# Low halves of the key and value weights made on GpSimd instead of VectorE, in a post-norm decoder layer on one core

## The reference, cut to what matters

```python
def _fp8_linear_pertensor(x, wq, w_scale, in_scale):
    xq = _div_clamp_fp8(x, in_scale)
    return jnp.einsum('bsi,oi->bso', xq * in_scale, wq) * w_scale
...
q = _fp8_linear_pertensor(ln_out, wq, wq_scale, q_in_scale).reshape(b, s, g, hpg, d)
k = _fp8_linear_pertensor(ln_out, wk, wk_scale, k_in_scale).reshape(b, s, g, d)
v = _fp8_linear_pertensor(ln_out, wv, wv_scale, v_in_scale).reshape(b, s, g, d)
...
qx = _fp8_linear_pertensor(ln_out, wqx, wqx_scale, qx_in_scale).reshape(b, s, g, hpg, d)
```

## Time and profile before

| | |
|---|---|
| median of 3 runs | 1780.35 us (1780.09 to 1781.36) |
| the profiled execution's own time | 1780.63 us |
| its span (first to last instruction) | 1778.5 us |
| PE / DVE / ACT / POOL busy | 98% / 79% / 62% / 15% of the span |
| granted TensorE clock | 0.997 of full speed over the span |
| one group in stage B (four pairs) | 153.17 us, of it PE busy 152.43 us |
| low halves, K and V, in stage B | 56 instructions of 0.34 us on DVE |

### The profile page before, as it was taken

One profiled execution on the slowest core, in us unless ns is written; L12 is line 12 of the kernel. 1 busy time (PEld: TensorE's weight loads), 2 busy tenths in 40 slices (PEclk: granted clock), 3 DMA queues, 4 the chain that ended last, 5 costly groups with the idle time before them and its releaser, 6 DMA issues.

```text
span 1778.5 us, 31332 instructions
## 1 busy us (share of the span) xinstructions
PE 1736.5 (98%) x10664; PEld 1180.9 (66%) x10664; DVE 1404.2 (79%) x4581; ACT 1103.9 (62%) x2378; POOL 273.9 (15%) x428
## 2 busy tenths in 40 slices
PE   9999999988999999999999999999999999989998
PEld 4454444666777777777777777777777777745453
DVE  1234526589888998998999899899889988879996
ACT  1252525375676767677776667767667665657775
POOL 0000000211121111112111111111111122101111
PEclk9999999999999999999999999999999999999999
DMA  8212200101101110121121012111101012000000
GB/s 284 83 59 83 71 24 26 37 1 50 50 19 42 45 62 19 44 68 36 33 67 32 19 44 67 37 44 55 32 19 44 32 48 97 1 1 19 25 25 30
DMA packets 45597, 83.30 MB, mean 47 GB/s; under 512 B 3585, under 2 KB 22529, under 8 KB 45057
## 3 DMA queue, kind: packets, MB, share of 16 engines
q1 hardware_dynamic: 45440, 81.31, 14.0%
HBM read 69.77 MB, written 10.49 MB: 45 GB/s over the span
## 4 chain that ended last, share of the span: by engine, by line
PE 63%; DVE 21%; issue 9%; ACT 3%; POOL 3%; DMA 1%; POOLq 0%; ACTq 0%
PE bank L536 13%; PE bank L602 9%; PE bank L648 8%; PE bank L701 5%; PE bank L626 4%; PE bank L737 3%; PE bank L455 3%; PE bank L493 3%; PE bank L581 2%; PE bank L407 2%; DVE nq L1250 2%; PE bank L434 2%; DVE nmx L1400 2%; DVE bnB L1226 2%; DVE pr L1260 2%
## 5 line engine op out<-in xcount | busy, mean ns | idle before, releaser
L536 PE MATMUL bank<-wqs,XQ 128*128 128x256 f16 x2048 | 246.4, 274 | 5.6 <-DVE x L1281 5.6
L602 PE MATMUL bank<-prT,KV 128*128 128x256 f32 x1024 | 245.3, 382 | 0.0
L648 PE MATMUL bank<-kT,qT 128*128 128x512 f32 x512 | 240.9, 593 | 0.0
L602 PEld LDWEIGHTS bank<-prT,KV 128*128 128x128 f32 x1024 | 189.3, 190 | 72.5 <-issue 51.9
L536 PEld LDWEIGHTS bank<-wqs,XQ 128*128 128x128 bf16 x2048 | 198.0, 99 | 47.7 <-DVE x L1281 21.1
L1020 ACT ACTIVATE pr<-bank,nmx 128x512 f32<-128x512 f32 x256 | 174.3, 687 | 57.4 <-DVE nmx L1400 56.0
L1569 POOL TENSOR_TENSOR rdev<-gvar,cst 128x7 f32<-128x7 f32 x128 | 193.1, 1509 | 10.0
L1567 POOL TENSOR_TENSOR gvar<-mvB,geps 128x7 f32<-128x7 f32 x128 | 30.7, 240 | 1040.2 <-DVE mvB L1240 1040.2
L1400 DVE TENSOR_REDUCE nmx<-bank 128x1 f32<-128x512 f32 x256 | 167.5, 682 | 9.6 <-PE bank L648 7.1
L821 ACT ACTIVATE prT<-bank 128x512 f32<-128x512 f32 x256 | 152.9, 613 | 26.7 <-PE bank L701 26.5
L701 PE MATMUL bank<-identf,pr 128*128 128x128 f32 x1024 | 151.6, 276 | 14.0 <-DVE pr L1260 11.0
(11 more groups left out here) (179 smaller groups left out, 3098.4 us busy)
## 6 DMA issues: line engine op xcount, KB each, us to landing
wst<-in_wcat SPq DMA_DIRECT2D x21, 512.0 KB, 4.0
nq<-in_wgu SPq DMA_DIRECT2D x16, 512.0 KB, 3.6
wpst<-in_wproj SPq DMA_DIRECT2D x8, 1024.0 KB, 6.3
wa<-in_wgu SPq DMA_DIRECT2D x16, 512.0 KB, 3.8
xT<-in_xT SPq DMA_DIRECT2D x4, 1024.0 KB, 7.7
nq<-in_wdn SPq DMA_DIRECT2D x8, 512.0 KB, 3.5
wkx<-in_wkvx SPq DMA_DIRECT2D x8, 512.0 KB, 4.9
tern_gu<-wa SPq DMA_DIRECT2D x16, 256.0 KB, 2.0
```

The source lines that it names most:

```text
L536: ins = mm(dst, XQ[:, b, c, k, j * P:(j + 1) * P], w, start=(k == 0 and m == 0), stop=(k == KT - 1 and m == 1))
L602: ins = mm(OB[:, 0:2 * P], KV[:, n % 2, t, P:2 * P], prT[:, st % 2, t, :, :].rearrange("p h s -> p (h s)"), start=(t == 0), stop=(t == ST ...
L648: mm(SB_[h][:], qT[:, h, st * P:(st + 1) * P], kT[:, :], start=True, stop=True).then_inc(s["scores_made"], 1)
```

## The change

DVE no longer makes any low half of K and V in stage B (parts 3g + 2 for g = 1 to 7; the three parts of group 0 are made ahead of the pairs on DVE as before). POOL makes them in pair b = 2, half 0 in step 2 and half 1 in step 3, each behind that step's `deviations`. POOL needs two instructions per tile where DVE needs one: a multiplication by `srel` in place in the staging buffer, then a subtraction of the fp16 high half into the fp16 low half. Between the four multiplications and the four subtractions stands a wait for its own instructions. Both engines raise the same count `wl_ready`.

```diff
--- before.py
+++ after.py
@@ DVE, pair @@
-                    if b == 2 and not last and st == 3:
-                        split_low(3 * (g + 1) + 2, 0)
                     if b in (1, 2) and not last and st == 1:
                         split_low(3 * (g + 1) + b - 1, 1)
                     if st == 0:
                         if T >= 2:
                             accumulate(T - 2, (4 * b - 2) % 16)
-                        if b and not last:
-                            split_low(3 * (g + 1) + b - 1, 1 if b == 3 else 0)
+                        if b in (1, 2) and not last:
+                            split_low(3 * (g + 1) + b - 1, 0)
@@ POOL @@
+            def split_low(part, half):
+                pool.wait_ge(s["wh_ready"], 2 * part + half + 1)
+                for c in WPART[part % 3]:
+                    for k in (2 * half, 2 * half + 1):
+                        own.do(g.tensor_scalar(staged(part, c, k), staged(part, c, k), srel[:, c, k:k + 1], None, ALU.mult))
+                own.sync()
+                for c in WPART[part % 3]:
+                    for k in (2 * half, 2 * half + 1):
+                        wh, wl = split_weights(part // 3, c, k)
+                        ins = g.tensor_tensor(wl, staged(part, c, k), wh, ALU.subtract)
+                ins.then_inc(s["wl_ready"], 1)
+
@@ POOL, pair @@
                     if nxt:
                         deviations(4 * n + 4 + st)
+                    if b == 2 and not last and st >= 2:
+                        split_low(3 * (gr + 1) + b, st - 2)
                     if T in XSTAT:
                         of_x(XSTAT[T])
```

## The result

The changed kernel takes 1775.94 us (median of 16 executions, 1774.54 to 1781.53) against 1780.36 us for the kernel before (16 executions, 1778.61 to 1784.74): ratio 0.9975, 95% interval 0.9968 to 0.9982. That is 0.25% or 4.4 us faster. A second measurement of the same code, further down, gave 0.9987 (0.9978 to 0.9996). The traces, whose pair times are steadier than the totals, show 3.7 us.

What follows compares the result with a forecast made beforehand. PE bounds the kernel, except where DVE's chain delays it ending pair b = 2. Gain min(0.58, 1.05 - 0.75) = 0.30 us per group, 7 x 0.30 = 2.1 us: 1778.2 us against the median 1780.35, range 1775.8 to 1788.0.

Steps and rivals of the forecast that it cites:

- Nothing is held: Rival: POOL's accesses slip between DVE's, up to 0.47 us delay per group; gain 4.2 us, 1776.1 us; chance 0.31.
- What bounds: End of pair b = 2: DVE's chain makes PE wait at L701; half 0 is on the path, half 1 covered.
- The cap: End of pair b = 2: gain limited by PE's idle 0.58 us per group, 4.2 us in all.
- some 0.7 us sooner: Pair b = 2: how much earlier pr ends, given the second nmx's wait for its score matmul and ACT's exponentials.
- the first rival: POOL's accesses slip between DVE's without holding it: gain 4.2 us, 1776.1 us; chance 0.31.
- d, the delay: DVE time lost to POOL's streams beside kn, pr, rounding: 0.75 us per group, bounds 0 and 3.5.
- nq's four follow each other too closely to be parted: Half 0, step 3: POOL's multiplications delay kn, pr and pr, 3 x 0.15 us, and not nq.
- POOL's sizes: POOL, each half: four multiplications of 0.29 us and four subtractions of 0.40, 2.8 us; 39 us over the kernel.
- cover: POOL time free before the next gvar: 4.0 us for half 0, 6.9 for half 1, against 2.8 needed.
- POOL's instructions are slow: Rival: from about 0.75 us each, rdev is late for nq; at 1 us each 8 us slower, 1788.5; chance 0.05.
- POOL holds the ports for a whole instruction: Rival: DVE blocked at nq, pr and rounding; at 1.8 us per group 5 us slower, 1785.5; chance 0.24.
- PE never waits for wlk: Next pair: half 1 is ready before PE's first wlk matmul at about 634.3, cover 6.9 us against 2.8.

Runs made afterwards that it cites:

- e3_half1_dve: Changed kernel with half 1 back on DVE in pair b = 3, step 0, half 0 staying on POOL: 1777.12 us, ratio 0.9985; pair b = 2 38.52 us.
- e2_half0_dve: Changed kernel with half 0 back on DVE in pair b = 2, step 3, half 1 staying on POOL: 1781.23 us, ratio 1.0002.
- e8_windows: Changed kernel, POOL started by DVE's progress: half 0 two wide instructions in step 3, half 1 four narrow multiplications and one wide subtraction: 1777.27 us, ratio 0.9980.
- e5_mult_tt: Changed kernel with POOL's multiplications as TENSOR_TENSOR, srel broadcast over the columns, instead of TENSOR_SCALAR: 1779.52 us (one execution); pair b = 2 39.16 us.
- e7_two_wide: Changed kernel with each half on POOL as two 128x512 instructions instead of eight of 128x128: 1792.89 us, ratio 1.0078.
- e4_sub_twice: Changed kernel with POOL doing the four subtractions of half 0 twice: 1780.3 us (one execution); pair b = 2 39.10 us.
- e11_after_again: The changed kernel measured again, nothing altered: 1778.33 us, ratio 0.9987 against the kernel before.
- e10_all_windows: Changed kernel, both halves as two wide POOL instructions started by DVE's progress, DVE's QX half 1 moved to step 0: 1774.39 us, ratio 0.9962.
- e6_mult_imm: Changed kernel with POOL's TENSOR_SCALAR multiplying by constant 1.0 instead of srel: 1776.94 us (one execution); pair b = 2 38.35 us.

## Why the prediction was right or wrong

The mechanism held; two of its sizes were off, and both errors made the gain too small. Forecast were 2.1 us, the traces show 3.7 and the first measurement 4.4. The result of 1775.94 us lies in the range by 0.14 us only and outside the forecast's own range (1776.6 to 1783.5); that it lies inside at all is partly luck, and so is the 0.7 us by which the first measurement exceeds the traces. It falls on the edge between the forecast and the rival "Nothing is held", whose edge was put at 0.54 us of delay per group; 0.53 or 0.54 were measured. But things are held: that rival's reason isn't what happened.

- **What bounds: right.** Only DVE's chain at the end of pair b = 2 was worth anything. Half 1's removal is worth nothing (e3_half1_dve has the full gain).
- **The cap: mis-sized.** The text had both limits: the second nmx that waits for the score matmul, "some 0.7 us sooner", and PE's idle time of 0.58, which it took because it was the smaller. The idle time understates what PE had to give (0.73 by the starts of L626 and L701), and the pair's cap was measured as 0.77. The forecast wasn't touched by it, the first rival was: with no delay at all the gain is 6 x 0.77 + (38.83 - 38.18) = 5.3 us, not 4.2.
- **d, the delay: mis-sized, and this is the term that decided.** Taken 0.75, measured 0.53. "nq's four follow each other too closely to be parted" failed: nq gave 0.26 of it, the largest part. pr gave 0.07 where two meetings at 0.15 stood. The rounding gave 0.21 for 0.2 forecast. Half 1 gave nothing for 0.1; where it meets nq at another distance it costs 0.10 to 0.14 (e2_half0_dve, e8_windows).
- **POOL's sizes: one right, one wrong.** The subtraction: 0.42 to 0.43 us for 0.40 forecast. The Trainium skill's "GPSIMD Engine Reference", section 3.1, had led to an estimate of 0.28 us for 128 columns of a two-input operation; the slopes below give 0.22 to 0.24, between that and the 0.20 taken. The multiplication: 0.71 for 0.29, taken from the affine select because that too has one tile in and one out. With one input it takes longer than with two, which no row before suggested. It did no harm: cover was 4.0 us, half 0 took 4.5, and behind the cover lay the slack of rdev, as the text had it. The rival "POOL's instructions are slow" named its point at 0.75 us for each instruction (by the cover of 4.0 and the slack of 2.8 us it would have been 0.85); the mean of the two kinds, (0.74 + 0.48) / 2 = 0.61, stayed under it.
- **"POOL holds the ports for a whole instruction": wrong for this kernel, right for one of its two instruction forms.** The changed kernel escapes it by accident. Its multiplications, which lie beside kn, nq and pr, are of the form that holds little (kn takes its usual 0.34 us wholly inside the first of them); its subtractions, of the form that holds all, mostly lie beside the statistics. e5_mult_tt exchanges the first form for the other, at the same distance from nq, and loses the gain; e7_two_wide makes the instructions long and is 0.78% slower. The Trainium skill's "SBUF — State Buffer", section "SBUF: two separate sides", says that of a VectorE instruction in a 2-port mode or with two SBUF inputs and a GpSimd one the first to start has the shared ports for the whole instruction; e7's kn (0.94 us, ending 0.08 us after POOL's) agrees for POOL's two-input instructions, but its first nq was held although its recorded start is 0.08 us ahead of POOL's; the changed kernel's nq (at most 473 ns beside multiplications of 599 ns and more) disagrees for the one-input form.
- **PE never waits for wlk**, as forecast. POOL, SP and PE at the end, from the timelines of the changed kernel:

```profile
629.48 2.00 POOL L1596 TENSOR_TENSOR wlk<-wst,whk 128x128 f16<-128x128 f32 x4
631.51 0.38 SPq L289 DMA_DIRECT2D wst<-in_wcat  x1
...
633.30 0.22 PE L536 MATMUL bank<-wlk,XQ 128*128 128x128 f16 x1
```

POOL is through at 631.48, PE's first matmul with the new wlk starts 1.8 us later. SP's load moves from 38.06 to 36.58 us into the pair, 1.5 us earlier and not 3 to 4, since the multiplications were longer. Nobody waits for it.

Left open is how a POOL TENSOR_SCALAR shares the ports with DVE. Both get longer when they meet (599 to 912 ns on POOL, 0.34 to at most 0.47 on DVE), and the price changes with the distance: the four nq take 1.11, 1.17, 1.25 or 1.37 us when the multiplications begin 0.29 (changed kernel, half 1), 0.13 (e4_sub_twice), 0.04 (e8_windows) or 0.41 us (changed kernel, half 0) ahead of them. The distance alone doesn't settle it: in the one pair of e11_after_again that strays they took 1.12 us at 0.41.

## What to carry to other kernels

Work moved from VectorE to GpSimd isn't priced by GpSimd's time but by what VectorE wants during it: here the same 4.4 us of GpSimd work a group cost VectorE's chain 2.9 us in one place (e7_two_wide) and nothing that could be seen in another (e10_all_windows). So look for the stretches in which VectorE reads PSUM, gathers statistics or waits, and let VectorE's own progress start the GpSimd instruction there. And measure an engine's stall from start to start against the same place in an undisturbed pair, since the idle time of a row leaves part of it out.

## What the runs showed of the hardware

- **GpSimd, 128x128 float32**: TENSOR_SCALAR 599 ns at least with a factor per row, 527 with a constant; TENSOR_TENSOR 392 ns with the factor repeated as a second input, 422 into fp16 from a tile and its fp16 partner. At 128x512 the last two take 1.05 and 1.15 us, so (1.05 - 0.39) / 384 = 1.7 and (1.15 - 0.42) / 384 = 1.9 ns for each further column. The Trainium skill's "GPSIMD Engine Reference", section 4.1, calls one-input operations roughly line-rate beside slower two-input ones; these rows show the one-input form as the slower.
- **A GpSimd TENSOR_TENSOR of 128x512 holds VectorE's kn and nq (TENSOR_SCALAR, SBUF to SBUF) until it is over.** In e7_two_wide kn took 0.94 us instead of 0.34 and one nq 1.31 instead of 0.34. The 7-column power, a TENSOR_TENSOR of 1.48 us, holds nothing that could be seen: beside it the rounding steps took their usual 0.29 and 0.42 us (e10_all_windows, 624.5 to 625.9 us).
- **It doesn't hold the head statistics, nmx or x.** In e10_all_windows, beside exactly the same instructions, they took 0.28, 0.69 and 0.74 us, as elsewhere, and nq stayed at 356 ns at most.
- **A GpSimd TENSOR_SCALAR of 128x128 holds them little or not.** In the changed kernel nq took 473 ns at most beside it, with a constant as factor 356 (e6_mult_imm).
- **Repeatability**: spans of one kernel differ by 3.3 us (before) and 3.7 us (after) between two profiles and medians of 11 to 16 executions by 2.4 us (1775.94 and 1778.33), pair durations by 0.02 us, but for the one stray of 0.10. For a change of 0.2% the pair is the measure.
